# First attention of a two-layer kernel: double-buffered parts, six pairs ahead, turned maxima as rows of the contraction

## The reference, cut to what matters

```python
xn = (x - mean) / sqrt(var + eps)                  # per token
q = xn @ Wq + bq;  k = ctx @ Wk + bk;  v = ctx @ Wv + bv   # 16 heads of 16
p = softmax(q @ k.T / 4)                           # per head, 256 x 256
x = x + tanh(g) * (concat(p @ v) @ Wo + bo)
```

## Time and profile before

| | |
|---|---|
| median of 3 runs | 967.94 us |
| profiled execution | 969.09 us, its span 967.3 us |
| TensorE busy | 840.8 us (87%) |
| VectorE busy | 712.1 us (74%) |
| ScalarE busy | 510.5 us (53%) |
| GpSimd busy | 77.6 us (8%) |
| maxima, L494 | 82.4 us, 128 of 687 ns |
| exponentials, L356 | 69.6 us, 128 of 597 ns |
| first attention | to about 214 us |

### The profile page before, as it was taken

The page is one execution under the profiler, slowest core; times in us unless marked ns, Lnnn a source line. Parts: engine busy times, 40 slices in busy tenths (PEclk is TensorE's granted clock), DMA queues, the critical chain, the costliest instruction groups (busy, mean ns, idle before and its releaser), DMA issues. The chain is left out here.

```text
span 967.3 us, 16700 instructions
## 1 busy us (share of the span) xinstructions
PE 840.8 (87%) x5552; PEld 674.0 (70%) x5555; DVE 712.1 (74%) x1608; ACT 510.5 (53%) x1067; POOL 77.6 (8%) x143
## 2 busy tenths in 40 slices
PE   4799999975577399999999999999899999995656
PEld 3667777643355278888888788888788888873223
DVE  4677888735665558888788698787688887774867
ACT  3366666633242155556556456555455565553765
POOL 3010101000400000000000000000000000000231
PEclk9699999987767799999999999999999999998788
DMA  7333222405000400000000000000000000001002
GB/s 143 112 106 99 95 92 75 135 4 184 0 1 0 112 10 12 1 12 1 2 12 1 3 13 1 1 12 2 3 12 1 1 1 1 1 1 31 1 0 87
DMA packets 37856, 33.33 MB, mean 34 GB/s; under 512 B 10224, under 2 KB 36528, under 8 KB 37520
## 3 DMA queue, kind: packets, MB, share of 16 engines
q1 hardware_dynamic: 37424, 31.76, 10.8%
q0 software_dynamic: 192, 0.39, 0.3%
q10 hardware_dynamic: 160, 0.13, 0.1%
HBM read 17.59 MB, written 2.10 MB: 20 GB/s over the span
## 5 line engine op out<-in xcount | busy, mean ns | idle before, releaser
L1388 ACT ACTIVATE c_probs<-c_pS,c_neg_max 128x512 f32<-128x512 f32 x128 | 88.0, 688 | 115.7 <-DVE c_neg_max L1510 115.7
L1510 DVE TENSOR_REDUCE c_neg_max<-c_pS 128x1 f32<-128x512 f32 x128 | 88.3, 690 | 66.2 <-PE c_pS L1711 64.3
L494 DVE TENSOR_REDUCE a_neg_max<-a_pS 128x2 f32<-128x512 f32 x128 | 82.4, 687 | 17.0 <-PE a_pS L645 16.4
L1505 DVE TENSOR_TENSOR c_pT_lo<-c_pT,c_pT_hi 128x512 fp32r<-128x512 f32 x128 | 87.1, 681 | 1.3 <-ACT c_pT_hi L1396 1.3
L356 ACT ACTIVATE a_probsT<-a_pT 128x512 f32<-128x512 f32 x128 | 69.6, 597 | 33.0 <-PE a_pT L661 32.1
L1728 PE MATMUL c_pO<-c_pT_hi,c_v_hi 128*128 128x256 f32 x256 | 77.4, 302 | 3.1 <-DVE c_pT_lo L1505 3.1
L1718 PE MATMUL c_pT<-ident,c_probs 128*128 128x128 f32 x512 | 77.2, 273 | 0.3 <-DVE c_probs L1517 0.3
L1718 PEld LDWEIGHTS c_pT<-ident,c_probs 128*128 128x128 f32 x512 | 63.7, 141 | 18.2 <-DVE c_probs L1517 0.8
L1401 ACT ACTIVATE c_oT<-c_pO,c_bv 128x256 f32<-128x256 f32 x64 | 30.3, 474 | 86.0 <-PE c_pO L1728 81.2
L1396 ACT CAST c_pT_hi<-c_pT 128x512 fp32r<-128x512 f32 x128 | 74.0, 579 | 0.0
L1728 PE MATMUL c_pO<-c_pT_hi,c_v_lo 128*128 128x256 f32 x256 | 72.0, 281 | 0.0
(11 more groups left out here) (347 smaller groups left out, 2155.7 us busy)
## 6 DMA issues: line engine op xcount, KB each, us to landing
a_q_stack<-a_q_parts SPq DMA_DIRECT2D x94, 64.0 KB, 2.6
a_k_stack<-a_k_parts SPq DMA_DIRECT2D x90, 64.0 KB, 2.6
a_ctx_in<-in_ctx_dram SPq DMA_DIRECT2D x8, 256.0 KB, 2.8
x_sb<-in_x_dram SPq DMA_DIRECT2D x8, 256.0 KB, 3.1
b_raw<-in_L_xattn_Wkv_dram SPq DMA_DIRECT2D x1, 2048.0 KB, 12.1
ctx_in<-in_ctx_dram SPq DMA_DIRECT2D x8, 256.0 KB, 2.7
out_dram<-x_sb SPq DMA_DIRECT2D x8, 256.0 KB, 2.2
b_raw<-in_L_xattn_Wq_dram SPq DMA_DIRECT2D x1, 1024.0 KB, 7.6
```

The costliest lines, as they stand in the source:

```text
L494: nc.vector.tensor_reduce(neg_max[:, r // 2 % 2, :, e, r % 2], pS[:, e, :, :], AX_X, ALU.max, negate=True).then_inc(s["max"], 1)
L1388: nc.scalar.activation(probs[:, u % 4, :], pS[:, u % 2, :], ACT.Exp, bias=neg_max[:, u % 4:u % 4 + 1], accum_out=sums[:, u % 4:u % 4 + 1]) ...
L1505: nc.vector.tensor_tensor(pT_lo[:, u // 2 % 2, :, half], pT[:, u % 2, :].rearrange("p (t q) -> p t q", q=P), pT_hi[:, u // 2 % 2, :, half] ...
L1510: nc.vector.tensor_reduce(neg_max[:, u % 4:u % 4 + 1], pS[:, u % 2, :], AX_X, ALU.max, negate=True).then_inc(s["max"], 1)
```

## The change

- `k_parts`, `q_parts` get two buffers; `high` waits for the stack of the batch before the last.
- `pick`, `mask` and the matmuls of L661 go. `k_stack` gets two further rows for each head, all ones, written once by two transfers at the start. The turned maxima in `shift` are copied into the same two rows of `q_stack` by two small transfers for each group from GpSimd's queue (`shift_in`). The shifted scores are one matmul over 50 rows and wait for these transfers.
- Scores, maxima, splits and turns run six pairs ahead of the shifted scores, not four (`AHEAD`).
- In the start the second query projection stands ahead of the first scores; two transfers of q's low part move from ScalarE's queue to GpSimd's, ahead of k's second half there.

```diff
-        k_parts = sb("a_k_parts", [P, 2, DC * T], F32R)
-        q_parts = sb("a_q_parts", [P, 2, DC * T], F32R)
+        k_parts = sb("a_k_parts", [P, 2, 2, DC * T], F32R)
+        q_parts = sb("a_q_parts", [P, 2, 2, DC * T], F32R)
...
+        AHEAD = 6
...
@@ gpsimd
+            pool.memset(unit[:, :], 1.0).then_inc(s["unit"], 1)
+            pool.wait_ge(s["unit"], 1)
+            for e in range(HP):
+                pool.dma_start(k_stack[64 * e + 3 * DK:64 * e + 3 * DK + 2, :, :, :].rearrange("p a r t -> p (a r) t").bitcast(F32),
+                               unit[:, None, :].broadcast_to([2, 2 * NR, T])).then_inc(s["units"], DMA)
...
+            def shift_in(G, g, par):
+
+                pause(pool, s["shift"], G + 1, s["pool_passed"])
+                for e in range(HP):
+                    pool.dma_start(q_stack[64 * e + 3 * DK:64 * e + 3 * DK + 2, par, 2 * g:2 * g + 2, :].bitcast(F32),
+                                   shift[64 * e:64 * e + 4, g % 2, :].bitcast(F32)).then_inc(s[("shifted0", "shifted1")[g % 2]], DMA)
...
             rstd_of(1)
             pool.wait_ge(s["zeros"], 1)
+            pool.wait_ge(s["q_lo"], 1)
+            place(pool, q_parts, q_stack, Q_ROWS[2:], 0, 0, s["first_q"])
             pool.wait_ge(s["k_lo"], 1)
...
+            place(pool, k_parts, k_stack, K_ROWS, 1, 0, s["first_k"])
             split_max(0, 0)
+            shift_in(0, 0, 0)
             split_max(1, 1)
+            shift_in(1, 1, 0)
+            split_max(2, 0)
 
             def batch(b, par, done, prep, more, old):
                 if prep:
                     rstd_of(b + 2)
-                for g in range(4 if more else 2):
-                    split_max(4 * b + 2 + g, g % 2)
+                shift_in(4 * b + 2, 2, par)
+                for g in range(3, 7 if more else 4):
+                    split_max(4 * b + g, g % 2)
+                    if g < 6:
+                        shift_in(4 * b + g, g % 4, par if g < 4 else 1 - par)
...
@@ scalar, high
-                wait(act, s["stack0"], HALF * n)
-                wait(act, s["stack1"], HALF * n - HALF // 2)
+                wait(act, s["stack0"], HALF * (n - 1) - 2 * DMA)
+                wait(act, s["stack1"], HALF * (n - 1) - HALF // 2)
...
@@ vector, batch
-                    if r < 4:
-                        pair_max(NR * b + r + 4, 4 * b + r // 2 + 2, r)
-                    elif more:
-                        pair_max(NR * b + r + 4, 4 * b + r // 2 + 2, r)
+                    if more or r + AHEAD < NR:
+                        pair_max(NR * b + r + AHEAD, 4 * b + (r + AHEAD) // 2, (r + AHEAD) % NR)
...
@@ tensor, shifted_scores
                 if r % 2 == 0:
-                    pe.wait_ge(s["shift"], G + 1)
+                    pe.wait_ge(s[("shifted0", "shifted1")[r // 2 % 2]], 2 * DMA * (2 * b + r // 4 + 1))
                 for t in range(TT):
                     for e in range(HP):
-                        rows = slice(64 * e, 64 * e + 3 * DK)
-                        nc.tensor.matmul(pT[:, e, t, :], k_stack[rows, par, r, t * P:(t + 1) * P], q_stack[rows, par, r, :], start=True, stop=False)
-                    for e in range(HP):
-                        rows = slice(64 * e, 64 * e + 64)
-                        last = nc.tensor.matmul(pT[:, e, t, :], pick[rows, r % 2, :], shift[rows, r // 2 % 2, :], start=False, stop=True)
+                        rows = slice(64 * e, 64 * e + 3 * DK + 2)
+                        last = nc.tensor.matmul(pT[:, e, t, :], k_stack[rows, par, r, t * P:(t + 1) * P], q_stack[rows, par, r, :], start=True, stop=True)
                 last.then_inc(s["ST"], 1)
...
@@ tensor, start
             project_k(1, 1, pP, (s["xT_lo"], 1))
+            project_q(1, pK, (s["k_lo"], 1))
             scores(0, 0, 0)
-            project_q(1, pK, (s["k_lo"], 1))
             scores(0, 0, 1)
             scores(0, 0, 2)
-            pe.wait_ge(s["pick"], 1)
             pe.wait_ge(s["vb"], 1)
+            turn_max(0, 0)
             scores(0, 0, 3)
-            turn_max(0, 0)
+            scores(0, 0, 4)
+            turn_max(1, 1)
+            scores(0, 0, 5)
+            pe.wait_ge(s["units"], HP * DMA)
             pe.wait_ge(s["k_lo"], 2)
             in_order(pe, batch)
```

More of the change, by code:

```diff
@@ L153, in attention0 @@
         pV = pb("a_pV", [P, 512])
-        names = """bias x0 x1 x2 x ident ident0 first gate load_k load_q load_v load_b load_g load_o ctx next wk wq wv scale
-                   const ones zeros mask pick stats moments var rstd xn cT cT_hi cT_lo xT xT_hi xT_lo k k_hi k_lo q q_hi
-                   q_lo stack0 stack1 v vb S max parts turned shift ST exp PV oT oQ rsum on onT onT_sb wo ob res
+        names = """bias x0 x1 x2 x ident ident0 first_k first_q gate load_k load_q load_v load_b load_g load_o ctx next wk wq wv scale
+                   const ones zeros unit units stats moments var rstd xn cT cT_hi cT_lo xT xT_hi xT_lo k k_hi k_lo q q_hi
+                   q_lo stack0 stack1 v vb S max parts turned shift shifted0 shifted1 ST exp PV oT oQ rsum on onT onT_sb wo ob res
                    dve_passed pool_passed sp_passed""".split()
@@ L174, in attention0, with place @@
         Q_ROWS = ((0, 0), (1, 0), (2, 1))
-        def place(eng, parts, stack, which, half, par):
+        def place(eng, parts, stack, which, half, par, done):
             for i, part in which:
@@ L180, in place @@
                     eng.dma_start(stack[64 * e + DK * i:64 * e + DK * i + DK, par, 4 * half:4 * half + 4, :].bitcast(F32),
-                                  parts[64 * e:64 * e + 64, part, half * T:(half + 1) * T].bitcast(F32)).then_inc(s[("stack0", "stack1")[half]], DMA)
+                                  parts[64 * e:64 * e + 64, par, part, half * T:(half + 1) * T].bitcast(F32)).then_inc(done, DMA)
+        AHEAD = 6
         block = ctx.enter_context(nc.Block())
@@ L197, in stacks @@
                     if later(n):
-                        pause(sp, s[("stack0", "stack1")[half]], HALF * n - half * HALF // 2, s["sp_passed"])
+                        pause(sp, s[("stack0", "stack1")[half]], HALF * n - (2 * DMA, HALF // 2)[half], s["sp_passed"])
                     if again:
@@ L343, in high, with k_high, q_high @@
                 last.then_inc(s[done], 1)
-            def k_high(n, bank=pK):
-                high(n, "k", k_parts, bank, bkq[:, 0, :], "k_hi")
-            def q_high(n, bank=pK):
-                high(n, "q", q_parts, bank, bkq[:, 1, :], "q_hi")
+            def k_high(n, par, bank=pK):
+                high(n, "k", k_parts[:, par, :, :], bank, bkq[:, 0, :], "k_hi")
+            def q_high(n, par, bank=pK):
+                high(n, "q", q_parts[:, par, :, :], bank, bkq[:, 1, :], "q_hi")
             def exps(n, G, r):
@@ L404, in _ @@
             act.wait_ge(s["bias"], 1)
-            k_high(0, pK)
+            k_high(0, 0, pK)
             xnT_hi(0, pP)
@@ L473, in low, with k_low, q_low @@
                 last.then_inc(s[done], 1)
-            def k_low(n, bank=pK):
-                low(n, "k_hi", k_parts, bank, bkq[:, 0, :], "k_lo")
-            def q_low(n, bank=pK):
-                low(n, "q_hi", q_parts, bank, bkq[:, 1, :], "q_lo")
+            def k_low(n, par, bank=pK):
+                low(n, "k_hi", k_parts[:, par, :, :], bank, bkq[:, 0, :], "k_lo")
+            def q_low(n, par, bank=pK):
+                low(n, "q_hi", q_parts[:, par, :, :], bank, bkq[:, 1, :], "q_lo")
             def v_out(n, par, bank=pK):
@@ L556, in _ @@
             norm_moments(1)
-            k_low(0, pK)
+            k_low(0, 0, pK)
             xnT_lo(0, pP)
@@ L636, in scores @@
                 if r == 0:
-                    pe.wait_ge(s["stack0"], HALF * b + HALF)
+                    pe.wait_ge(s["stack0"], HALF * b + HALF - 2 * DMA)
                 if r == 4:
                     pe.wait_ge(s["stack1"], HALF * b + HALF // 2)
-                if isinstance(b, int) and b == 0 and r == 4:
-                    pe.wait_ge(s["first"], HALF // 2)
+                if isinstance(b, int) and b == 0 and r in (0, 4):
+                    pe.wait_ge(s[("first_q", "first_k")[r // 4]], (2, 6)[r // 4] * DMA)
                 for t in range(TT):
@@ L722, in batch @@
                         group(b, par, r // 2 - 1)
-                    if r % 2 == 0 and (more or r < 6):
-                        turn_max(4 * b + r // 2 + 1, (r // 2 + 1) % 2)
+                    if r % 2 == 0 and (more or r < 4):
+                        turn_max(4 * b + r // 2 + 2, r // 2 % 2)
                     if r == 1 and more:
```

80 lines of the change are left out of this document (35 added, 45 removed).

## The result

The changed kernel takes 960.36 us (median of 5 runs, 957.58 to 962.63), the kernel before 967.39 (966.20 to 969.95 in the same job): ratio 0.9923, 95% interval 0.9897 to 0.9948. Timed again on another chip it was 959.61 against 967.80, ratio 0.992 (0.9897 to 0.9943). The forecast was 957, from 950 to 965. The time lies in that range; several terms of the sum did not come true.

What follows compares the result with a forecast made beforehand. It took TensorE, busy throughout mid-attention, as the bound, with VectorE and ScalarE chains limiting some steps. Gains summed to 11.0 us, 969.09 to 958.1, a median of 956.9; forecast 957, from 953 to 960, 8 in 10 within 950 to 965.

Steps and rivals of the forecast that it cites:

- Part 1: First attention's loop: pick and shift matmuls go; a steady batch gains 0.69 us instead of 1.92, other chains holding the rest.
- T(0): Start of step 0's shifted scores in a batch; forecast at 34.0 us in batch 0, then 21.4 apart in steady batches.
- S(1): Start of the plain scores behind step 1's shifted scores; forecast to be released by VectorE's maximum in steady batches.
- Rival A: Loop and start: removed time comes through whole, TensorE stays the bound; 18.9 us gained, 950 us; chance 0.10.
- Part 3: Start and batch 1: parts in two buffers, second projection early; T(2) 2.7 us earlier, 0.5 us gained in batch 1.
- steps 0 and 1 save 0.42 each at the low clock: Batch 0: each of its first two steps saves 0.42 us without pick matmuls while the clock is 1.2 GHz.
- the clock full from about 40: Sign in batch 0: TensorE's clock back at its full 2.4 GHz from about 40 us.
- the 1.56 forecast: Gain in batch 1: steady 0.69, 0.37 for steps 0 and 1, and 0.5 from ScalarE's wait for parts.
- rival C: Start and loop: lighter TensorE work and new waits let the clock fall; slower, 980 us with four such batches; chance 0.07.
- Part 4: GpSimd's queue carries turned maxima: 1.1 us issue per group, 5 us to last landing; cost 0, up to 1 in batch 7.
- batch 6's forecast 1.44: Batch 6 gains 0.48 in steps 0 and 1, 0.24 in each middle pair, 0.48 in steps 6 and 7.
- Rival B: Loop: GpSimd's issues or landings take twice the assumed value and TensorE waits at even steps; 966 us; chance 0.13.

Runs made afterwards that it cites:

- the doubled pass: Changed kernel with each half pass of the shifted scores made twice, giving TensorE back the pick matmuls' time: 968.03 us, ratio 1.0005.
- the other order: Changed kernel with VectorE taking the maxima before out_bias, statistics, moments, normalisation and q's low part in their steps: 955.27 us, ratio 0.9861.
- the fills: 40 idle transposes of ident around the first six scores, added to the changed kernel with late weight loads and VectorE's new order: 949.38 us, ratio 0.9823.

## Why the prediction was right, and where it was not

**Part 1, the loop: right.** T(0) to S(1) in batch 3 is 3.46 us (102.05 to 105.51), to the hundredth the chain forecast not to shorten. S(1) and S(5) are released by VectorE's maximum (105.51 and 116.00 above), VectorE is busy 20.84 of 25 us ("nearly 21"), and the batches are 21.49 us apart where 21.37 was worked out from 22.06 less 0.69. 0.57 us of 1.92 come through. By pairs of steps the gain is 0, 0.48, 0 and 0.09 us, forecast 0, 0.48, 0 and 0.21; the missing 0.12 lie in steps 6 and 7, where S(7) to T(0) takes 2.35 us instead of 2.25. That the loop's gain is TensorE's time is shown by the doubled pass (22.01 to 22.07), that VectorE's chains hold the rest by the other order (20.95), and that the queue and the deeper run ahead matter to neither by the kernel without L661 (21.47). Rival A is out. (Its price was added up wrong: 967.94 less 18.9 is 949.0, not 950; and the start's bounds and 1 us for the chains give 954.5 to 959.5 and not 953 to 960.)

**Part 3, the start: right up to T(0), wrong behind it.** S(0) 22.66 for 22.5, S(1) 24.55 for "about 2 us later", T(0) 34.18 for 34.0; in the two other profiles T(0) is at 35.02 and 34.92, inside the bounds but with half of the 1.88 us forecast. T(2) came at 41.59 for 40.1, since T(0) to T(2) took 7.41 us where 6.1 was assumed. Two things were wrong there. The first is the term "steps 0 and 1 save 0.42 each at the low clock": they take 7.28 to 7.45 us with the single pass (four profiles) and 7.49 with the doubled one (two), all at 1.2 GHz, so the pass is worth at most 0.2 us over both steps, not 0.84. In step 0 the scores wait for VectorE's maximum (0.19 us at 35.17); the 6.94 us of the kernel before, from which the term was taken, had the full clock again for their last 0.7 us. The second is "the clock full from about 40": it was at 1.2 GHz from 26.3 to 43.4 in the changed kernel, with TensorE waiting 0.8 to 1.4 us ahead of each of the scores from 24.55 to 32.99 us and gapless only from about 35. The steps up to there ran at half speed, so batch 0 lost 0.45 where a gain of 1.54 was forecast. What the fills bring from S(0) to T(3), 2.0 us, is what this clock costs, as far as it is shown.

**Batch 1: wrong by 3.3 us in the first profile.** It was 24.38 us long, 22.93 and 23.00 in the two others, against 22.65 and 23.22 before: a gain of about nothing for the 1.56 forecast. This was rival C, priced as a whole (22 us) and given 0.07 for it; it came small. During the third of three waits of 0.56, 0.28 and 0.60 us in 2.5 us the granted clock fell at 57.1 us for 6.8 us, and step 0 took 5.17 us instead of 3.03. Part of it is no clock: with L661 alone left out steps 0 and 1 of batch 1 ran at the full clock and took 6.05 us, before 5.98, so the 0.37 us forecast for them were not there. The fall adds 1.5 us (3.4 us at half clock, both repeats) to 3.0 us (6.8 us, first profile) to these 6.05.

Six profiles have one pass per shifted score and VectorE's old order. In five of them the clock fell at these three waits or up to 1.1 us behind them: at 57.1, 58.0 and 58.1 in the changed kernel, 59.0 with the weight loads late, 53.9 with two buffers and no L661. In the sixth, L661 alone left out, it did not, and fell at 71.6 behind waits of 1.08 and 0.64. In none of the eight others did it fall in batch 1: before twice, two buffers alone, the doubled passes twice, VectorE's other order three times. That several waits close together bring the clock down there is thus supported from two sides, TensorE filled and the waits removed. It is no rule: the sixth profile passed the same three waits, and single waits of 2.02, 1.43 and 2.22 us at T(0) of batch 7 (changed twice again, doubled in two batches) were followed by no fall, one of 1.94 us was. The steady batches, with two waits of 0.3 and 0.5 us some 10 us apart, keep 1.00.

**Part 4, GpSimd's queue: right in the loop, wrong at one place.** 560 ns an issue as in the earlier trace rows and 579 at most, so VectorE's normalisation held none up, 1.12 us a group, and landing in 2.3 us at the median, less than the 3.8 taken; in the start, where the 3.8 had been read, up to 4.5. The prediction gave the last batch half a microsecond of cover and looked only at GpSimd's side. It did not ask what else is in the DMA engines at that time: six weight loads that SyncE issues from 175.25 on, 179 to 185 us at 325 to 341 GB/s and a DMA share of 1.00 to 1.04, the same loads as before (DMA share 0.53 in both kernels from 168 to 188 us), where no small transfer stood behind them. A group behind them landed in 6.3 us, and TensorE waited 1.94 us and, in this profile alone, then ran at half clock for 3.4. Of batch 6's forecast 1.44 this left -0.46; with the loads held back batch 6 takes 17.25 us, before 18.78, a gain of 1.53. So this term was right but for the wait. Rival B, in the form of its landings and not of its issues; moving the loads removes it. The Trainium skill ("DMA: Bandwidth & Descriptors", section "Queues, rings and completion order") says that each DMA engine takes turns between the queues that have work, a packet at a time; from that alone one might expect 4 KB to slip through between the loads. The trace shows no such thing: 5.5 and 6.3 us behind the loads, 1.7 at the same place with the loads held back.

**The sum: inside the range, in part by luck.** Forecast 11.0 us, median gain 7.0 and 8.2. In the stage the three profiles give 2.8, 3.7 and 5.0 against the mean of the two of before (216.6), 3.8 on the mean, a third of the forecast, because the start behind T(0), the clock in batch 1 and the stall in batch 6 took some 7 us back (1.99 + 3.29 + 1.90 in the first profile, forecast less measured). Another 1.0 is in batch 7, where this profile ran at half clock from 186.8 to 190.2; without that fall T(0) to the last T takes 12.6 us (late loads, both repeats), before 14.3, 1.7 of the 1.85 forecast. The mean from the next stage on is 750.4 in before's two and 747.8 in the changed kernel's three, about 3 us less, with a scatter of 5.5 us among the latter. This goes with the time at 1.2 GHz there; two profiles against three can't tell whether it is chance, and these 3 us of the gain stay without a shown cause. With the stage's 3.8 us alone the time would be 963.6, still inside the range but near its upper end.

## What to carry to other kernels

Taking work off the bound engine is worth only the steps in which no other chain ends within that amount: read the time between the last maximum and the matmul it frees, step by step, and sum those. A small transfer put on the critical path must be looked up against everything else in the DMA engines at its time, not against its own queue alone; hold bulk loads back until the last of the small ones is in. Running further ahead has a price in the start: two more scores cost some 3.5 to 4 us here and brought 0.6 at the end. A faster engine that now waits shortly several times may lose its clock, which costs more here (1.5 to 3.0 us in two steps) than each step gained (0.24). Profiles with the same start differ by up to 1.3 us at the first scores already, so measure what an edit brings from an event ahead of it that both profiles have.

## What was not expected of the hardware

- A 4 KB transfer from SBUF to SBUF, issued by GpSimd, lands in 1.6 us at the least and 2.3 at the median (64 transfers); behind the weight loads of another queue the slowest took 5.4 to 6.6 us in six profiles, and once in 7.3 beside loads of 256 KB.
- Issue on GpSimd costs 560 ns for 4 KB on 4 rows, 567 for 64 KB: the size hardly enters.
- Contraction over 50 rows is as fast as over 48: a pass is 0.50 us for four matmuls in both, and the steady batch agrees with that of the kernel without L661 to 0.02 us.
- The granted clock went down at 57.1 us with no wait of TensorE longer than 0.60 us just ahead of it, and stayed full behind single waits of 1.43 to 2.22 us in three profiles.
